# The second half's softmax shift moved forward in three queues of a fused attention and feed-forward kernel

## What is computed

```python
xn = _layernorm(x, axis=-1)
x = x + _L0_attn_ref(xn, ...) + _L0_ffn_ref(xn, ...)
# attention, 16 heads of 8 features
q = jnp.einsum('bsd,hde->bhse', x, wq) + bq        # k and v alike
scores = jax.nn.softmax(jnp.einsum('bhse,bhte->bhst', q, k) * scale, axis=-1)
att = jnp.einsum('bhst,bhte->bhse', scores, v)
# feed-forward: xr, xk mix each token with the one before it
r = jax.nn.sigmoid(jnp.einsum('btc,dc->btd', xr, W_r))
k_act = jnp.square(jax.nn.relu(jnp.einsum('btc,dc->btd', xk, W_k)))
out = r * jnp.einsum('btc,dc->btd', k_act, W_v)
```

## Time and profile before

| | |
|---|---|
| time, median of 3 runs | 506.4 us (506.03 to 507.11) |
| the profiled execution | 506.4 us, span 504.6 us |
| busy share of the span | PE 90%, DVE 84%, ACT 77%, POOL 68% |
| mean granted clock of TensorE | 0.997 |
| DMA engines | mean 120 GB/s |
| one item in the middle (252.56 to 266.81 us) | 14.25 us, with PE busy 13.70, DVE 13.02, ACT 12.07, POOL 10.60 |
| an item with the loop's turn (266.81 to 281.60 us) | 14.79 us |

### The profile page before, as it was taken

One profiled execution on the slowest core, in us unless ns is written; L12 is line 12 of the kernel. 1 busy time (PEld: TensorE's weight loads), 2 busy tenths in 40 slices (PEclk: granted clock), 3 DMA queues, 4 the chain that ended last, 5 costly groups with the idle time before them and its releaser, 6 DMA issues.

```text
span 504.6 us, 15503 instructions
## 1 busy us (share of the span) xinstructions
PE 454.6 (90%) x5184; PEld 259.1 (51%) x5184; DVE 422.8 (84%) x882; ACT 389.2 (77%) x833; POOL 342.6 (68%) x615
## 2 busy tenths in 40 slices
PE   1388999899999999999999999999999999999995
PEld 1134555555555555555555555555555555555552
DVE  4297899889898999899998999989998999988831
ACT  1107888788888888888888888888888888888883
POOL 6656777677786777777876777678776777776220
PEclk9999999999999999999999999999999999999998
DMA  2442455344544443345444444454444434544200
GB/s 83 125 137 78 126 139 144 109 114 126 149 132 134 136 126 112 110 137 147 126 137 136 126 117 115 127 147 131 133 137 124 122 112 127 147 132 114 76 16 21
DMA packets 85837, 60.43 MB, mean 120 GB/s; under 512 B 6192, under 2 KB 73392, under 8 KB 85808
## 3 DMA queue, kind: packets, MB, share of 16 engines
q1 hardware_dynamic: 85808, 60.06, 42.2%
HBM read 29.89 MB, written 29.36 MB: 117 GB/s over the span
## 4 chain that ended last, share of the span: by engine, by line
PE 47%; DMA 14%; SPq 10%; issue 10%; POOL 8%; DVE 8%; ACT 2%; DVEq 0%; ACTq 0%; POOLq 0%
PE bank_exp L567 13%; PE bank_val L535 13%; DMA ops<-shift 12%; DVE neg_max L473 6%; SPq L236 5%; SPq L221 5%; PE bank_max L572 4%; PE misc_b L638 4%; POOL act_sq L327 4%; POOL qk_m L329 3%; PE misc_c L658 3%; PE misc_a L646 3%; PE misc_b L662 2%; PE misc_a L668 2%; ACT probs L399 1%
## 5 line engine op out<-in xcount | busy, mean ns | idle before, releaser
L473 DVE TENSOR_REDUCE neg_max<-bank_max 128x2 f32<-128x512 f32 x512 | 330.0, 687 | 47.4 <-PE bank_max L572 43.7
L399 ACT ACTIVATE probs<-bank_exp 128x512 f32<-128x512 f32 x512 | 279.3, 596 | 57.9 <-PE bank_exp L567 57.6
L567 PE MATMUL bank_exp<-ops 51*128 51x256 bf16 x1024 | 165.8, 271 | 22.6 <-DMA ops<-shift 17.8
L572 PE MATMUL bank_max<-ops 48*128 48x256 bf16 x1024 | 170.8, 278 | 10.6 <-DMA ops<-spill 8.1
L535 PE MATMUL bank_val<-probs,val 128*25 128x256 f32 x2048 | 136.3, 384 | 1.2 <-ACT probs L399 1.2
L567 PEld LDWEIGHTS bank_exp<-ops 51*128 51x128 bf16 x1024 | 66.1, 94 | 111.0 <-issue 60.7
L535 PEld LDWEIGHTS bank_val<-probs,val 128*25 128x25 f32 x2048 | 50.4, 103 | 51.8 <-issue 26.8
L572 PEld LDWEIGHTS bank_max<-ops 48*128 48x128 bf16 x1024 | 62.2, 95 | 18.3 <-DMA ops<-spill 8.5
L361 POOL TENSOR_TENSOR rstd<-var_eps,minus_half 128x2 f32<-128x2 f32 x32 | 22.9, 714 | 48.0 <-DVE var_eps L503 45.4
L317 POOL TENSOR_SCALAR xn<-x_in,moments,rstd 128x128 f32<-128x128 f32 x64 | 50.7, 798 | 0.1
L356 POOL TENSOR_TENSOR mixed_x<-mixed_x,xn_t 128x512 f32<-128x512 f32 x32 | 40.8, 1275 | 2.5
(11 more groups left out here) (59 smaller groups left out, 596.6 us busy)
## 6 DMA issues: line engine op xcount, KB each, us to landing
ops<-spill SPq DMA_DIRECT2D x128, 192.0 KB, 3.4
spill<-qk_h SPq DMA_DIRECT2D x64, 192.0 KB, 3.4
spill<-qk_m SPq DMA_DIRECT2D x64, 128.0 KB, 1.9
x_in<-x SPq DMA_DIRECT2D x32, 128.0 KB, 2.2
spill<-qk_l SPq DMA_DIRECT2D x32, 128.0 KB, 1.9
y_out<-y SPq DMA_DIRECT2D x32, 128.0 KB, 1.9
ops<-shift SPq DMA_DIRECT2D x128, 6.0 KB
w<-weights SPq DMA_DIRECT2D x1, 448.0 KB, 3.1
```

Source lines behind the costliest of these rows:

```text
L399: nc.scalar.activation(probs[g % 2][:, u % G, :, :], bank_exp[u % 2][:, :, :], ACT.Exp, scale=SCALE).then_inc(exp_done[u], 1)
L473: nc.vector.tensor_reduce(out=neg_max[hf][:, :, r, pr], in_=bank_max[v % 2][:, :, :], axis=AX_X, op=ALU.max, negate=True).then_inc(max_don ...
L567: exp_mm = nc.tensor.matmul(bank_exp[r][:, i, :], ops[p][rows, hf, 1, pr, i * P:(i + 1) * P], ops[p][rows, hf, 0, pr, :], start=True, stop ...
L572: max_mm = nc.tensor.matmul(bank_max[r][:, i, :], of[rows, max_hf, 0, max_pr, i * P:(i + 1) * P], of[rows, max_hf, 1, max_pr, :], start=Tr ...
```

## The change

The second half's shift is moved forward in three queues, and nothing is added or removed. PE's two transposes (with their waits) go in front of `mix_values(3)`. ACT's copy `move_shift(1)` goes from behind unit 3 to behind unit 1, in front of the copy `mixed`. SP's two DMAs `load_shift(1)` go in front of the two spills of the m part.

```diff
@@ sync
                     spill_part(p, "h", qk_h, h_done, n)
-                if live(2):
-                    spill_part(p, "m", qk_m, (m_done, m_done), n)
                 if live(0):
                     load_shift(1, p, n(0), moved(-1, 2))
                 if live(2):
+                    spill_part(p, "m", qk_m, (m_done, m_done), n)
                     spill_l(p, n)
@@ scalar
+                    if u == 1 and live(0):
+                        move_shift(1, n(0), moved(-1, 2))
                     if u == 1 and live(-1):
                         act.wait_ge(mix_psum[NG - 1], n(-1))
                         nc.scalar.copy(mixed[:, :, :], bank_val[:, :, :]).then_inc(mixed_done, 1)
                     if u == 3 and live(0):
-                        move_shift(1, n(0), moved(-1, 2))
                         act.wait_ge(gate_psum, n(0))
@@ tensor
-                    if u == 1 and live(-1):
-                        mix_values(3, n(-1), n(-2), 1 - p)
                     if u == 1 and live(0):
                         pe.wait_ge(max_split[1], n(0))
                         pe.wait_ge(shift_done[0], n(0))
                         after(pe, qk_rest_done[0], n(2))
                         transpose_shift(1)
+                    if u == 1 and live(-1):
+                        mix_values(3, n(-1), n(-2), 1 - p)
```

## The result

The changed kernel takes **495.27 us** (median of 4 runs, 494.49 to 495.61) against 506.75 us (506.03 to 508.6) for the kernel before in the same comparison. The ratio on record is 0.9765 (the quotient of the two medians is 0.9773), with a 95% interval of 0.9742 to 0.9788: 2.35% faster. Every median here is over fast runs; of all runs only one was slow, of the version with the shift's loads behind the spill of l (696.68 us at a granted clock of 0.58), and it is left out. The profiled execution took 495.58 us with a span of 493.8 us, 10.8 us less on either count than before.

A forecast was written before the change was run, and what follows sets the result against it. PE's unit 8 waits for the second half's shift, tied by SP's order to the m part; 0.29 gained less 0.04 lost is 0.25 us per item, 30 items 7.5 us, 506.4 to 498.9 us; own range 496.2 to 503.1, wider 494.5 to 503.5.

The forecast's parts named there:

- Unit 9 cannot: PE's unit 9 must await DVE's reduction of unit 7, so it starts 0.34 us earlier, unit 8 up to 0.55.
- Rival A: At unit 8 PE gets all its wait back, 0.55 us per item, 16.5 us in all, 489.9 us; chance 0.08.
- The prediction's own sign: Length of an item in the middle: 14.0 us where it was 14.25; near 13.8 would mean all the wait returned.
- near misses of A: Gains such as 0.39 us per item, short of PE's whole wait at unit 8, counted inside the range 494.5 to 503.5.
- DVE starts unit 8 at 264.22, right behind the statistics: DVE's unit 8 in step 15: 264.22 against 264.51, a gain of 0.29 us per item.
- 0.04 us lost: PE's transposes in front of unit 1's value products delay unit 3 by 0.04 us per item, range 0 to 0.18.
- The bound of 30 x 0.34: Upper bound of the gain, 0.34 us in each of 30 items: 10.2 us, giving 496.2 us.
- over 1 us earlier: In SP's queue the spill of l and the first half's reload come over 1 us earlier.
- Rival B: The shift is held up behind the h spills, or reloads come late at unit 6 or 14: 506.4 us; chance 0.05.
- C: PE's transposes in front of the value products cost more than the wait was worth: 513.3 us; chance 0.06.
- D: ACT's new order delays the copy mixed, its transposes and unit 4; at 0.7 us the gain is gone, 506; chance 0.05.
- The rule on the rings: On the DMA rings the shift's loads land with the second h spill, at 261.7 instead of 261.5, both before unit 8.

The follow-up runs named there:

- the second kernel: The kernel before with PE's and ACT's parts of the change alone, SP's order kept: 506.25 us, ratio 0.9994.
- the reciprocal's move: The changed kernel with DVE's reciprocal of the denominators moved from behind unit 5's reduction to behind unit 3's: 487.27 us; same edit on the kernel before: 507.17 us.
- three kernels: Kernel before with SP's part alone, 503.17 us; changed kernel with ACT's part undone, 505.54 us; changed kernel with two idle DMAs behind the shift's loads, 505.06 us.

## Why the prediction was right, and where it was off

**The place and the direction** were right. The wait of unit 8 was an effect of SP's order and no part of the shift's own way. SP's part alone brings unit 8 to 6.61 us, as early as in the changed kernel, and the second kernel shows it from the other side: the shift copied early, with SP's order kept, gains nothing.

**The next limit** was right. "Unit 9 cannot" start as early as unit 8 was the step that cut the 0.55 us of idle time down. Unit 9 came 0.34 us earlier, to the hundredth what the text worked out from unit 7's reduction, and the reciprocal's move confirmed the reduction as the limit. Rival A, all of the wait, did not happen: unit 8 gained 0.62 us and the item 0.36. The prediction's own sign would not have told this: it took 14.0 us for an item as its forecast and 13.8 as A, and 13.89 lies between the two. (A's own sum gives 14.25 - 0.55 = 13.70 for an item.) What speaks against A is the place of unit 9 and the reciprocal's move.

**The size** was off, 7.5 us forecast and 11.1 measured against the 506.4 us that it started from (11.5 in the comparison above). At 495.27 us the result lies 0.9 us below the forecast's own range of 496.2 to 503.1. It is inside the wider range only because that one went down to 494.5, for near misses of A, and no term of the sum leads there; that much is luck. Two terms were mis-sized:

- "DVE starts unit 8 at 264.22, right behind the statistics ... 0.29 us earlier, and from there PE's second unit of each pair follows DVE". I took the end of the statistics' record and a handover behind it. Records of neighbouring DVE instructions overlap: the reduction starts 0.39 us after the statistics begin, not 0.50, so it came 0.40 us earlier, not 0.29. And moving the statistics away changed nothing, so what follows does not hang on DVE's start at unit 8. The gain of unit 9, 0.34, was the number to carry on, and the rest of the item kept it: 0.36.
- "0.04 us lost" at unit 1. The loss is 0: unit 2 starts 1.62 us after unit 0 against 1.63, unit 4 at 3.30 in both. The transposes delay the value products in front by about 0.1 us and no longer stand in their drain. With PE's part undone the time is the same within the runs.

0.36 in place of 0.25 us, 30 times, is 3.3 us, nearly all of the miss of 3.6; the 1.0 us more that the early items gained and the 1.0 us that the end lost cancel. The bound of 30 x 0.34 in the text gave 496.2, 1 us from the result.

**A cover that I did not name.** The text let the reload of the first half come "over 1 us earlier" and gave it no value. The runs show that this is what ACT's part is for. With the reload at 8.0 us instead of 6.6 most of the gain is lost again at unit 14 (503.2 to 505.5 us in three kernels). Rival B had the mechanism in half a sentence ("make the reloads late at unit 6 or 14"), but without its price, about 8 to 10 us, and without the remark that the kernel before had 0 to 0.36 us of slack in it.

**Rivals C and D.** Against C speak unit 2 at 1.62 us and the kernel with PE's part undone. Against D: ACT's copy mixed moved back against unit 0 (1.77 us instead of 1.67), and unit 4 did not. The rule on the rings, by which the small loads land no sooner than the h spills before them, mattered to no unit: the second load landed 0.85 us or more before unit 8 in every item. Its landing took 1.90 to 2.74 us from its issue, where the kernel before had 1.90 to 1.93 in every item, so behind the h spills it is up to 0.8 us later than the sum had it. But it did not always come with the second h spill, as the prediction's form of the rule has it: in the item that starts at 236.58 it landed 4.59 us after unit 0 and the second h spill at 4.76. The rule speaks of each DMA engine by itself, and that these totals don't decide.

## What to carry to other kernels

A DMA that the critical engine waits for should not stand in a queue behind one that waits for something slower; but see what its wait then holds up behind it. Moving the issue alone paid a third of the gain here, because it waited in the queue in front of spills that were ready, and a reload farther on had no slack: a queue entry should be moved together with what it waits for. And when a wait goes, read which neighbour of it is bound by whom, start to start rather than by the ends of records; the gain is the least of these, and the place where it stops is the next edit (one reciprocal, another 8 us).

## What the runs showed that I had not expected

Three edits that bring 11.5 us together bring 3.8 and 0.7 us in two groups: gains of moves in coupled queues don't add. A late reload shows up in the trace of PE as idle time put down to "issue" (8.8 to 12.9 us), not as a wait for the DMA that was late, so it has to be found by offsets within an item and by the landings, 0.09 us before the unit that waited. And the same reciprocal is worth 8.0 us after the change and nothing before it.
